# New instruction orders for all five engines of a decoder layer: list scatters in lumps, additions and gathers in turn

## The reference

```python
# 1. attention with a latent of L = 72, H = 16 heads, causal
xn = layernorm(x);  kv = xn @ latent_w + latent_b
q = einsum('btc,hcl->bhtl', xn, Wd_w) + Wd_b
y = softmax(mask(q @ kv.T / 4)) @ kv
x1 = x + reshape(y) @ out_w + out_b
# 2. bidirectional RWKV mix of the context, gated by the normalised x1
wkv = (Af + Ab + cur * v) / (Bf + Bb + cur)      # scans over the 128 tokens, both ways
x2 = x1 + sigmoid(layernorm(x1)) * wkv
# 3. mixture of experts: 8 experts, each token goes to its best two
sel, w = sparsemixer(layernorm(x2) @ router_w.T)
out = x2 + sum over both choices of w * (silu(h @ gate[e]) * (h @ up[e])) @ down[e]
```

## Time and profile before

| what | value |
|---|---|
| median of 3 runs | 599.59 us (596.92 to 600.35) |
| the profiled execution | 605.2 us, its span 603.6 us |
| TensorE busy | 525.9 us (87%) |
| VectorE / ScalarE / GpSimd busy | 359.3 (60%) / 329.1 (55%) / 321.8 us (53%) |
| mean granted TensorE clock | 0.954 |
| DMA | 76.82 MB, mean 127 GB/s |

### The profile page before, as it was taken

How to read it: one execution, slowest core, us unless ns; L and a number is a source line. 1 busy time by engine, 2 the same in 40 slices (tenths; PEclk the granted TensorE clock), 3 DMA queues, 4 the chain that set the end, 5 groups by cost and what they waited for, 6 DMA issues and landing times.

```text
span 603.6 us, 10367 instructions
## 1 busy us (share of the span) xinstructions
PE 525.9 (87%) x3448; PEld 456.3 (76%) x3448; DVE 359.3 (60%) x740; ACT 329.1 (55%) x947; POOL 321.8 (53%) x277
## 2 busy tenths in 40 slices
PE   1799998999999899997999976999899999589881
PEld 1687776877777787886776756989899899589780
DVE  3756899665875685634556646777657766422010
ACT  5557766667567566652571636554667465533120
POOL 4744677445674327745475575075654653744332
PEclk9999999999999999999996986897999999799987
DMA  6532122122314122214052059536978878499700
GB/s 216 182 106 59 46 90 84 61 63 76 105 48 129 38 63 66 83 39 132 26 156 61 22 163 318 164 95 124 293 188 240 213 184 277 89 284 264 237 9 0
DMA packets 53219, 76.82 MB, mean 127 GB/s; under 512 B 10173, under 2 KB 41662, under 8 KB 52838
## 3 DMA queue, kind: packets, MB, share of 16 engines
q1 hardware_dynamic: 43322, 65.09, 34.1%
q0 software_dynamic: 9040, 10.93, 9.3%
q10 hardware_dynamic: 804, 0.15, 0.1%
HBM read 49.28 MB, written 9.49 MB: 97 GB/s over the span
## 4 chain that ended last, share of the span: by engine, by line
PE 31%; DMA 17%; issue 12%; POOL 11%; DVE 11%; ACT 10%; SPq 3%; another core or an unknown queue 1%; POOLq 1%; ACTq 0%; DVEq 0%
DMA out<-Y,TK 13%; PE P L770 9%; PE P L850 4%; PE P L833 4%; PE PO L878 4%; POOL EB L1695 3%; ACT EB L1085 3%; POOL out L1779 3%; PE P L841 3%; DMA xs<-TKS,SL 2%; PE P L954 1%; PE P L894 1%; DVE ZT L1314 1%; DVE small L1299 1%
## 5 line engine op out<-in xcount | busy, mean ns | idle before, releaser
L1695 POOL TENSOR_TENSOR EB<-EB,small 128x512 f32<-128x512 f32 x64 | 77.0, 1209 | 95.7 <-DVE small L1303 95.5
L770 PE MATMUL P<-GT,WF 128*128 128x256 f32 x768 | 103.6, 297 | 5.7 <-DVE GT L1234 3.3
L1779 POOL DMA_INDIRECT out<-Y,TK x39 | 65.8, 1688 | 78.7 <-DMA out<-Y,TK 38.5
L770 PEld LDWEIGHTS P<-GT,WF 128*128 128x128 f32 x768 | 100.5, 205 | 7.0 <-DVE GT L1234 3.7
L1085 ACT ACTIVATE EB<-P,small 128x128 f32<-128x128 f32 x256 | 90.6, 379 | 27.1 <-DVE small L1299 22.5
L1090 ACT ACTIVATE PT<-P 128x512 f32<-128x512 f32 x64 | 38.7, 605 | 75.9 <-PE P L841 55.5
L833 PEld LDWEIGHTS P<-KT,qT 72*128 72x128 f32 x512 | 67.9, 193 | 5.1 <-issue 1.9
L850 PE MATMUL P<-PT,V 128*72 128x512 f32 x128 | 68.7, 619 | 2.4 <-DVE ZT L1314 2.2
L833 PE MATMUL P<-KT,qT 72*128 72x128 f32 x512 | 68.3, 277 | 0.0
L1314 DVE COPY ZT<-P 72x512 f32<-72x512 f32 x64 | 43.1, 673 | 41.1 <-PE P L850 36.1
L878 PE MATMUL PO<-Ow,zP 128*128 128x256 f32 x270 | 67.1, 389 | 0.0
(11 more groups left out here) (235 smaller groups left out, 941.9 us busy)
## 6 DMA issues: line engine op xcount, KB each, us to landing
WR<-wf SPq DMA_DIRECT2D x27, 512.0 KB, 4.7
arena<-wf SPq DMA_DIRECT2D x24, 512.0 KB, 5.9
qT<-qP SPq DMA_DIRECT2D x72, 128.0 KB
WS<-wf SPq DMA_DIRECT2D x12, 512.0 KB, 8.3
zP<-ZT SPq DMA_DIRECT2D x80, 72.0 KB
zP<-ZT SPq DMA_DIRECT2D x80, 36.0 KB
X<-x SPq DMA_DIRECT2D x4, 512.0 KB, 6.7
cxa<-ctxin SPq DMA_DIRECT2D x4, 512.0 KB, 5.0
```

The source lines that it names most:

```text
L770: r = e.matmul(o, lt(a), rt_(b), start=start and n == 0, stop=stop and n == 2, skip_group_check=skip)
L1695: e.tensor_tensor(EB[i][:, :, :], EB[i][:, :, :], SM[i].unsqueeze(2).broadcast_to([128, 4, 128]), ALU.mult).then_inc(s_prob, 1)
L1779: e.indirect_dma_start(outr, bass.IndirectOffsetOnAxis(ap=TK[:, j, a_, 0:1].bitcast(i32), axis=0), Y[j % 2][:, a_, :], None, bounds_check= ...
```

## The change

The five tables of the engines are replaced by other orders of the same steps. No step is added or removed, `STEPS` and all functions stay. Of the diff a few rows of GpSimd's table show its form:

```diff
 GPSIMD_STEPS = """
-    r4.3.0.4.1.2 ao.0 lxg.5 lxg.6 lxg.7 lxg.8 lxg.9 ao.1 lxg.10 ao.2 ao.3 lxg.11 ao.4 ao.5 ao.6 lxg.12 lxg.13 lxg.14 ao.7 ao.8 lxg.15 ao.9 ao.10
+    r4.3.0.4.1.2 ao.0 lxg.5 ao.1 lxg.6 lxg.7 ao.2 lxg.8 lxg.9 ao.3 lxg.10 ao.4 lxg.11 ao.5 lxg.12 ao.6 ao.7 lxg.13 ao.8 lxg.14 ao.9 lxg.15 ao.10
```

More of the change, by code:

```diff
@@ L185 @@
 SYNC_STEPS = """
[L186 to L193, removed]
@@ L194 @@
-    lw.20.2 lw.21.2 lw.21.0 lw.22.1 lw.22.0 lw.22.2
+    ctx.0 q.0.0 q.0.1 q.0.2 q.0.3 q.0.4 q.1.0 q.1.1 ctx.1 q.1.2 q.1.3 q.1.4 Y.1 Y.3 q.2.0 q.2.1 Y.5 Y.7 q.2.2 q.2.3 q.2.4 ctx.2 Y.9 Y.11 Y.13 Y.15
+    q.3.0 q.3.1 Y.17 q.3.2 q.3.3 q.3.4 q.4.0 q.4.1 Y.19 ctx.3 Y.21 Y.23 q.4.2 q.4.3 q.4.4 Y.25 xd.0.0.4 Y.27 Y.29 Y.31 q.5.0 q.5.1 q.5.2 Y.33 q.5.3
+    out.0.0.4 q.5.4 q.6.0 Y.35 q.6.1 Y.37 Y.39 q.6.2 q.6.3 q.6.4 q.7.0 Y.40 Y.41 Y.42 Y.43 Y.44 Y.45 Y.46 Y.47 xd.1.0.4 q.7.1 Y.48 q.7.2 q.7.3 q.7.4
@@ new lines @@
+    Y.49 Y.50 owh out.1.0.4 Y.51 Y.52 Y.53 Y.54 Y.55 Y.56 Y.57 Y.58 Y.59 ltk.3 ltk.4 xd.2.0.4 lw.1.1 lw.2.1 lw.1.2 xd.3.0.2 lw.2.0 lw.1.0 xd.3.2.2
+    lw.2.2 lw.3.0 out.2.0.4 out.3.0.2 out.3.2.2 lw.3.1 lw.3.2 lw.4.1 lw.4.0 lw.5.0 lw.6.0 ltk.5 ltk.6 lw.5.1 lw.6.1 lw.4.2 lw.5.2 ltk.7 ltk.8 ltk.9
+    lw.7.0 lw.6.2 lw.7.1 lw.8.0 lw.8.1 ltk.10 ltk.11 ltk.12 ltk.13 lw.7.2 lw.9.0 lw.9.1 ltk.14 lw.10.1 lw.8.2 lw.10.0 lw.11.1 lw.9.2 lw.10.2 lw.11.0
+    ltk.15 lw.12.1 ltk.16 lw.12.0 lw.13.0 lw.11.2 lw.12.2 ltk.17 ltk.18 lw.13.1 lw.14.1 lw.13.2 lw.14.0 ltk.19 ltk.20 ltk.21 lw.15.0 lw.15.1 lw.17.0
@@ L216 @@
+    up.16.0 up.17.0 dn.15 tg.18 tg.19 up.18.0 dn.16 dn.17 tg.20 up.19.0 tg.21 tg.22 up.20.0 dn.18 dn.19 dn.20 up.21.0 up.22.0 dn.21 dn.22
 """
 VECTOR_STEPS = """
-    bn.1.0.0.0 bn.1.0.0.2 agg.1.0.0.4 nmb.1.0.0.4 split tx.1.0.0.4.0 tx.1.0.0.4.1 bn.1.1.0.0 bn.1.1.0.2 consts agg.1.1.0.4 nmb.1.1.0.4 w1.0.0 w2.0.0
-    w3.0.0 w4.0.0 w5.0.0 w1.0.1 w8.0.0.0 w8.0.0.1 w2.0.1 w8.0.0.2 w8.0.0.3 S.0 S.1 w3.0.1 vb.0 tx.1.1.0.4.0 N.0 S.2 S.3 N.1 N.2 N.3 w8.0.1.0 S.4 S.5
-    Y.0 w8.0.1.1 Y.1 w4.0.1 tx.1.1.0.4.1 bn.1.2.0.0 N.4 Y.2 w5.0.1 S.6 N.5 N.6 Y.3 S.7 S.8 w1.1.0 w2.1.0 w3.1.0 N.7 bn.1.2.0.2 Y.4 N.8 agg.1.2.0.4 S.9
@@ L242 @@
-    hd.12.1 sw.13.1 sw.14.1 sw.12.2 sh.12.0 sh.12.1 hd.13.0 sh.13.0 sw.15.0 tg.14 tg.15 hd.13.1 sw.13.2 sw.15.1 hd.14.0 sh.13.1 sh.14.0 sw.14.2
-    hd.14.1 sh.14.1 hd.15.0 hd.15.1 sw.15.2 sh.15.0 sh.15.1 hd.16.0 hd.17.0 hd.18.0 hd.19.0 hd.20.0 hd.21.0 hd.22.0
+    bn.1.0.0.0 bn.1.0.0.2 agg.1.0.0.4 nmb.1.0.0.4 split tx.1.0.0.4.0 tx.1.0.0.4.1 consts bn.1.1.0.0 bn.1.1.0.2 agg.1.1.0.4 w1.0.0 w2.0.0 w3.0.0
+    nmb.1.1.0.4 w4.0.0 w5.0.0 w8.0.0.0 w1.0.1 w8.0.0.1 w8.0.0.2 w2.0.1 w3.0.1 S.0 w4.0.1 S.1 w5.0.1 N.0 w8.0.0.3 N.1 S.2 vb.0 S.3 tx.1.1.0.4.0 N.2 N.3
@@ new lines @@
+    agg.2.2.0.4 Y.49 nr.2.0.4 S.54 Y.50 x2.2.0.0.0 S.55 x2.2.0.2.0 bn.3.2.0.0 Y.51 N.53 N.54 S.56 Y.52 S.57 bn.3.2.0.2 N.55 agg.3.2.0.4 nmb.3.2.0.4
+    Y.53 N.56 r3.1.0.4 rw.1.0.4 Y.54 S.58 S.59 N.57 N.58 lgc.2.0.4 Y.55 r1.2.0.4 r2.2.0.4 ra.2.0.4 Y.56 S.60 S.61 r3.2.0.4 N.59 Y.57 N.60 rw.2.0.4
+    N.61 Y.58 p1.0 p2.0 p3.0 Y.59 add.6 bn.2.3.0.0 agg.2.3.0.2 S.62 S.63 nr.3.0.2 N.62 Y.60 x2.3.0.0.1 bn.3.3.0.0 agg.3.3.0.2 N.63 Y.61 Y.62 Y.63
+    sw.0.1 nmb.3.3.0.2 sw.0.0 add.7 bn.2.3.2.0 agg.2.3.2.2 nr.3.2.2 tg.0 x2.3.2.2.1 bn.3.3.2.0 agg.3.3.2.2 nmb.3.3.2.2 sw.0.2 sw.1.2 sw.1.1 tg.1
@@ new lines @@
+    S.8 T.6 S.9 q.2.1 q.2.2 T.7 S.10 q.2.3 w1.1.1 q.2.4 T.8 S.11 T.9 S.12 kt.1 q.3.0 wb.0.0 S.13 xn.1.2.0.0 T.10 T.11 w2.1.1 S.14 S.15 q.3.1 wb.0.1
+    w4.1.1 T.12 S.16 T.13 xn.1.2.0.2 T.14 T.15 S.17 wb.1.0 w1.2.0 T.16 S.18 S.19 tx.1.2.0.4.0 q.3.2 T.17 q.3.3 w2.2.0 w4.2.0 S.20 q.3.4 S.21
+    tx.1.2.0.4.1 T.18 w1.2.1 w2.2.1 T.19 T.20 S.22 q.4.0 S.23 T.21 S.24 q.4.1 S.25 T.22 w4.2.1 q.4.2 sig.0.0.0 sig.0.0.2 T.23 q.4.3 q.4.4 T.24 S.26
+    S.27 kt.2 T.25 S.28 S.29 T.26 T.27 q.5.0 wb.1.1 S.30 xn.3.0.0.0 xn.3.0.0.2 T.28 T.29 S.31 w1.3.0 T.30 S.32 q.5.1 S.33 tx.3.0.0.4.0 tx.3.0.0.4.1
```

128 lines of the change are left out of this document (62 added, 66 removed).

## The result

| | before | after |
|---|---|---|
| median | 599.88 us (596.92 to 600.35, 4 runs) | 580.75 us (579.95 to 582.98, 4 runs) |
| profiled execution, span | 605.2, 603.6 us | 580.73, 579.0 us |
| TensorE busy, mean granted clock | 525.9 us, 0.954 | 511.8 us, 0.969 |
| GpSimd busy | 321.8 us | 314.0 us |

The ratio is 0.968 (95% interval 0.965 to 0.972): 19.1 us faster by the medians. The two spans differ by 24.5 us, since the profiled execution of before was 5.3 us over its median.

A forecast was written before the change was run, and what follows sets the result against it. TensorE was taken to bound attention, chained output additions the experts. Terms -2.5, -8, -4.5, -3.7 made a walk of 19 us; +3.5 and +4.5 left -11, span 592.6, scaled to 589 us; range 582 to 596 (0.50), wider 578 to 604.

The forecast's parts named there:

- a walk of 19: Going down the new orders from 309 us with the trace's durations; it gave 19 us before anything was taken back.
- What bounds the kernel: Attention is held by TensorE, the expert part by output additions waiting for landings, 9.40 us a tile; TensorE's pace nearly equal.
- so they can hardly get better and easily worse: +4.5, my choice: Reordered attention ahead of 309 us, with TensorE busy 48.4 of 50 us: 4.5 us taken back from the gain.
- The walk to the gate: End of attention: units 59 to 61 scaled together, scatters behind them; first gate product 2.5 us earlier.
- The lump: Rival: eight scatters on GpSimd between units 61 and 62 delay additions 8 us, 608 us; chance 0.18 with other new stops.
- The stall of 3.5 us: VectorE stood 4.2 us near 318 unexplained; such a stop will be somewhere, so 3.5 us taken back.
- First expert tiles: Earlier normalisation, router, lists and tile 1's weighting bring tile 3's down product from 425.81 to near 415.3: -8 us more.
- Additions: Fewer gathers ahead of GpSimd's additions: -4.5 us at tile 3's addition, -3.7 us at tile 7's, tables alike from tile 8.
- Scans and splits against issues: Moving VectorE work away from GpSimd's issues could win 0 to 3 us; none taken beyond the walk.
- The signs named ahead: Observations to show the forecast right or wrong: unit 61 before 331 us, tile 3's addition at 431 to 436, others.
- Loads: Rival: weight loads hold TensorE and the additions from tile 3 on; around 598 us, chance 0.18 for loads or drift.
- The full walk: Rival: the walk holds with nothing taken back, 19 us off, 581 us; chance 0.14 for under 582.

The follow-up runs named there:

- early_tiles: two_edits plus the new TensorE, ScalarE and VectorE orders from the end of attention to about tile 1's down product; 600.96 us, ratio 1.001 to before.
- after_weigh1_late: Kernel after with tile 1's weighting on ScalarE moved 17 steps later, just ahead of tile 2's; 579.47 us, ratio 0.969 to before.
- after_old_start: Kernel after with the old orders of all five engines up to unit 52 (about 290 us); 584.82 us, ratio 0.976 to before.
- two_edits: Kernel before with GpSimd's new table from tile 0's additions on and tile 1's weighting right behind tile 0's on ScalarE; 600.88 us, ratio 1.001.

## Why the prediction came out as it did

| step | predicted | by the traces |
|---|---|---|
| first gate product | -2.5 | -8.3 (363.19 to 354.88) |
| from there to tile 3's down product | -8 | -7.1 |
| from there to tile 3's addition | -4.5 | -5.5 |
| from there to tile 7's addition | -3.7 | -0.3 |
| from there to the end | 0 | -3.3 |
| taken back for a stall and a worse attention | +8 | 0 |
| span | -11 | -24.5 |

The traced execution of before was 5.3 us over its median, so the second column holds 5.3 us that no change of order made, and a row of it can be off by some of them. By the medians 19.1 us were gained. The range of 578 to 604 us held this by its width and in part by luck. The forecast took 8 us off a walk of 19, which nothing in the traces bears out, and -8.3 stands where the walk had -2.5.

**What bounds the kernel** was read rightly for before. The end follows tile 3's addition at a fixed distance, as the last column of the experiments' table shows, and the kernels without additions are 27 to 37 and 19 to 21 us faster. That the additions alone set this distance isn't shown: TensorE has nearly the same pace, as the prediction said itself, and in after the chain of waits is TensorE's to 510 us.

**The step that failed is "so they can hardly get better and easily worse: +4.5, my choice".** It rests on 48.4 of 50 us at 200 to 250 us. Over 50 to 300 us there were 14.0 us to win, and 7.6 were won; without unnamed waits it is 12.3 (early_tiles) against 6.4 (after_weigh1_late). With the term at 0 the prediction's sum would have been -15.2 us. The part of this that can be named is small waits: TensorE's weight loads for the transposes waited 10.7 us in all for GpSimd's scaling between 50 and 300 us, and wait 5.8 now. The rows of before, then of after (us in total, times, longest):

```profile
PEld P L841 <- POOL EB L1695: 10.7, 13, 1.7
```

```profile
PEld P L841 <- POOL EB L1695: 5.8, 10, 1.0
```

**The walk to the gate** had unit 61's scaling done near 326.4 and the gate 2.5 us earlier. The scaling was done at 316.4 (three units in 3.03 us from 313.37), 10 us ahead of the walk, since the walk kept the times before 309 us: the six scatters that began at 309.15 in before ended at 310.79 in after. Unit 63 went at 338.48, not near 347. The lump of 8 x 1.27 us took 316.56 to 326.4 and was hidden, as its rival's own condition (before 331) said. So the term of -2.5 us was mis-sized: the gate came 8.3 us earlier, and the walk's moves at the end of attention don't give this by themselves: behind the old start the new end costs 4.5 us (after_old_start).

**The stall of 3.5 us** was the right kind of thing at the wrong size. Before's profile has four waits that nothing explains, 7.03, 4.22, 3.46 and 3.42 us, and a fifth of 3.97 beside the last; after's has three, 3.49, 11.45 and 6.02. Their sum is 18 (22 with the fifth) and 21 us, so they take back little by the difference. In traces without them attention ends 9.2 us earlier with after's orders and 5.9 with before's (early_tiles).

**First expert tiles** were as forecast: lists at 377.05 and 15.4 us earlier at tile 3's down product, 8.3 of it attention's. But the cause was told as single moves that add up, and they don't. two_edits and early_tiles have the two moves on which I put most of it, and neither gains a measurable time; they need the rest of the new orders with them. Which part of the rest, SyncE's loads or the later steps of the other engines, no run parts.

**Additions**: tile 3's -4.5 us came as -5.5, though its start, 425.35 us, was 6 us ahead of the forecast 431; the term of -3.7 at tile 7 was mis-sized. Six gathers ahead of tile 7 were no loss once the tiles ahead had room: 37.88 us from tile 3 to tile 7 before, 37.56 now. Nearly the same amount came where nothing was expected: from tile 15 to tile 16 it took 11.48 us and takes 7.85; TensorE's idle time of 6.62 us at 520.12 is gone. The tables also differ behind tile 8, which the prediction took to be alike: three gathers stood between the additions of tiles 10 and 11, and one stands there now.

**Scans and splits against issues**: nothing was taken, and nothing came. The issues of the additions in after (ns shortest/median/longest) against 1578 ns:

```profile
L1779 POOL DMA_INDIRECT out<-Y,TK x39: 1547/1605/2352, 393.2 to 570.0; - x39
```

The reading that gather issues are long beside weight splits holds. The 19 gather issues of after that overlap a split of a weight part on VectorE have a median of 1.19 us and take up to 2.04, the 20 others have 1.00 and take up to 1.06 (in before 20 with 1.21, up to 2.86, and 19 with 0.97, up to 1.40).

**The signs named ahead.** Unit 61 before 331 us, 9.40 us a tile, no wait of ScalarE for a load near 424 us and the idle time near 520 gone: all four came. Tile 3's addition at 431 to 436 did not, it was earlier. Of the signs of being wrong one came by half: TensorE was idle 3.72 us at 314.01, but the clock up to 250 us was 1.00.

**The rivals.** Loads don't hold the tiles: no wait of ScalarE for a load is over 5 us in after (4.96 at 485.03, the longest). The lump is hidden. The full walk came, but by other parts than its own: attention's -8.3 for -2.5, and the experts' 16.2 us, which equal the walk's 8, 4.5 and 3.7 in sum and not each by each. That it gave the measured time is in part luck.

## What to carry to other kernels

Read the idle time of the engine that bounds over the whole phase before calling it full: five stretches of 50 us, not one of the best. Where one chain sets the end (here additions that each wait for the landing of the last), find its first link that moves with the end, and forecast that link; then ask of the other engines whether they keep the same pace. When orders of several engines change together, moving one engine's part is no measure of its share: here the gathers alone cost 1.2%, two of the key edits gave nothing measurable, and all the new orders but two rows of GpSimd's table gave nothing either.
